# Softmax rows scaled on GpSimd: from a broadcast tensor operand to a per-partition scalar operand

## The reference

```
xn = layernorm(x)                                    # x: 4 x 512 x 256
s  = attention(xn)      # 16 heads of 128, 4 K/V heads, causal softmax, Wo, gelu, + xn, layer norm, gamma, beta
g  = silu(ffn(xn))      # gate and up 256 -> 1024, silu(gate) * up, down 1024 -> 256
out = x + s * g

scores = Q K^T / sqrt(128) + mask                    # mask: -1e9 above the diagonal
attn   = softmax(scores)                             # exp(scores - max) / sum
ctx    = attn V
```

## Time and profile before

| | |
|---|---|
| median of 3 runs | 715.47 us (715.37 to 715.48) |
| the profiled execution | 716.74 us |
| its span, first to last instruction | 714.9 us |
| PE busy | 671.6 us, 94% of the span |
| DVE / ACT / POOL busy | 480.0 / 433.2 / 279.7 us |
| granted TensorE clock, mean | 0.989 of full speed |

### The profile page before, as it was taken

One profiled execution on the slowest core, in us unless ns is written; L12 is line 12 of the kernel. 1 busy time (PEld: TensorE's weight loads), 2 busy tenths in 40 slices (PEclk: granted clock), 3 DMA queues, 4 the chain that ended last, 5 costly groups with the idle time before them and its releaser, 6 DMA issues.

```text
span 714.9 us, 11581 instructions
## 1 busy us (share of the span) xinstructions
PE 671.6 (94%) x3968; PEld 585.2 (82%) x3968; DVE 480.0 (67%) x1620; ACT 433.2 (61%) x1011; POOL 279.7 (39%) x328
## 2 busy tenths in 40 slices
PE   1889999999999999999999999999999999999982
PEld 1778888888888888897888888888888897888872
DVE  6764433334776777777868776786768677867777
ACT  3423232326767677668767675867767677767661
POOL 2599100000524324146815242484425146715234
PEclk9799999999999999999999999999999999999998
DMA  8334000002000000000110000002000000200000
GB/s 275 119 129 136 1 29 0 30 0 85 5 1 1 1 0 1 1 1 1 56 34 2 1 1 0 2 1 89 1 1 1 1 1 1 89 1 2 1 1 29
DMA packets 14503, 20.31 MB, mean 28 GB/s; under 512 B 752, under 2 KB 12144, under 8 KB 14192
## 3 DMA queue, kind: packets, MB, share of 16 engines
q1 hardware_dynamic: 13328, 14.37, 6.1%
q0 software_dynamic: 1120, 5.24, 2.2%
HBM read 15.41 MB, written 4.19 MB: 27 GB/s over the span
## 4 chain that ended last, share of the span: by engine, by line
PE 86%; DVE 7%; ACT 4%; issue 1%; DMA 1%; SPq 0%; DVEq 0%; ACTq 0%
PE bank L949 30%; PE down_ps L949 28%; PE down_ps L1048 8%; PE down_ps L987 6%; PE bank L974 6%; PE bank L976 6%; DVE cT_lo L822 2%; PE bank L1035 2%; ACT cT_hi L702 2%; DVE hidT_lo L766 1%; DMA raw<-in_wgu 1%; DVE pT_lo L804 1%; DVE xnT_lo L751 1%; ACT L655 1%; ACT res L655 0%
## 5 line engine op out<-in xcount | busy, mean ns | idle before, releaser
L561 POOL TENSOR_TENSOR probs<-probs,inv 128x512 f32<-128x512 f32 (+3 forms) x256 | 180.7, 720 | 385.0 <-DVE inv L907 384.9
L692 ACT ACTIVATE probs<-probs,least 128x512 f32<-128x512 f32 (+3 forms) x256 | 142.2, 558 | 40.5 <-DVE least L900 36.8
L900 DVE CUSTOM_DVE_ANT_0 probs<-bank,mask 128x512 f32<-128x512 f32 (+3 forms) x256 | 121.2, 486 | 12.1 <-issue 12.0
L804 DVE TENSOR_TENSOR pT_lo<-down_ps,pT_hi 128x512 fp32r<-128x512 f32 x156 | 107.1, 687 | 20.0 <-ACT pT_hi L698 15.4
L698 ACT ACTIVATE pT_hi<-down_ps 128x512 fp32r<-128x512 f32 x156 | 92.5, 593 | 33.1 <-PE down_ps L1048 31.1
L1048 PE MATMUL down_ps<-ident,probs 128*128 128x128 f32 x624 | 93.4, 272 | 0.0
L1048 PEld LDWEIGHTS down_ps<-ident,probs 128*128 128x128 f32 x624 | 75.5, 140 | 12.4
L949 PE MATMUL down_ps<-wo_lo,cT_hi 128*128 128x256 f32 x256 | 73.7, 288 | 6.0 <-DVE cT_lo L822 6.0
L816 DVE SCALAR_TENSOR_TENSOR qT_lo<-bank,bias,qT_hi 128x512 fp32r<-128x512 f32 x64 | 47.5, 750 | 43.5 <-ACT qT_hi L685 43.5
L949 PE MATMUL down_ps<-pT_lo,v_hi 128*128 128x512 f32 x156 | 67.8, 435 | 5.6 <-DVE cT_lo L822 4.2
L949 PE MATMUL down_ps<-wo_hi,cT_lo 128*128 128x256 f32 x256 | 72.0, 281 | 0.0
(11 more groups left out here) (139 smaller groups left out, 1547.6 us busy)
## 6 DMA issues: line engine op xcount, KB each, us to landing
x_row<-in_x SPq DMA_DIRECT2D x4, 512.0 KB, 6.8
raw<-in_wgu SPq DMA_DIRECT2D x4, 512.0 KB, 6.1
raw<-in_wq POOLq DMA_DIRECT2D x2, 1024.0 KB, 5.1
raw<-in_wo POOLq DMA_DIRECT2D x2, 1024.0 KB, 6.2
g_scratch<-g_out SPq DMA_DIRECT2D x4, 512.0 KB, 2.9
x_b<-in_x SPq DMA_DIRECT2D x4, 512.0 KB, 3.7
g_b<-g_scratch SPq DMA_DIRECT2D x4, 512.0 KB, 4.7
out<-res SPq DMA_DIRECT2D x3, 512.0 KB, 2.9
```

The costliest lines, as they stand in the source:

```text
L561: nc.gpsimd.tensor_tensor(p, p, inv[:, u % UNITS, g:g + 1].to_broadcast([P, (tile_of(u) + 1) * P]), ALU.mult).then_inc(probs_made, 1)
L692: nc.scalar.activation(p, p, ACT.Exp, bias=least[:, u % UNITS, g:g + 1], scale=-1.0, accum_out=total[:, u % UNITS, g:g + 1]).then_inc(exp_ ...
L804: nc.vector.tensor_tensor(lo[:], ps, f32(hi[:]), ALU.subtract).then_inc(probsT_split, 1)
L900: nc.vector.tensor_tensor_reduce(out=probs[t][:, g, :], in0=ps[:, 0:(t + 1) * P], in1=mask[:, (T - 1 - t) * P:], scale=-SCALE, scalar=BIG, ...
```

## The change

POOL's multiplication at L561 took `inv` as a second tensor of the same shape as the probabilities, a 128 x 1 column read again and again (`to_broadcast`). It becomes an instruction with one tensor input and `inv` as a scalar for each partition. Its place in POOL's list, its wait and its semaphore stay. Each of the 256 instructions changes in this way, and no other instruction of any engine.

```diff
                     p = probs[tile_of(u)][:, g, :]
-                    nc.gpsimd.tensor_tensor(p, p, inv[:, u % UNITS, g:g + 1].to_broadcast([P, (tile_of(u) + 1) * P]),
-                                            ALU.mult).then_inc(probs_made, 1)
+                    nc.gpsimd.tensor_scalar(p, p, inv[:, u % UNITS, g:g + 1], None, ALU.mult).then_inc(probs_made, 1)
```

## The result

The changed kernel takes 723.14 us in the median of 8 runs, the kernel before, timed beside it, 716.63 us (8 runs). The ratio is 1.0096 with a 95% interval of 1.0059 to 1.0132. The two sets of runs do not overlap: 722.1 to 728.7 us now, 715.4 to 721.1 before. The likeliest case of the prediction, no change at 715.5 us, was wrong; what happened is its rival 1, which had a chance of 0.38, and its range, 714.6 to 738, holds the time.

What follows compares the result with a forecast made beforehand. PE was taken to bound the kernel, POOL being in time by 0.18 us at twelve tile-3 transposes. All terms were 0: profiled 716.74 us + 0, which lies 1.27 over the median, so 715.5 us; range 714.6 to 738 us.

Steps and rivals of the forecast that it cites:

- likeliest case of the prediction: Whole kernel: POOL's multiplications get no dearer, nothing on the path changes, 715.5 us; chance 0.50.
- rival 1: Tile-3 transposes: PE waits for POOL if 512 columns cost over 1.29 us; 728.3 or 736.2 us; chance 0.38.
- the price of the new instruction: POOL's multiplication at L561, 512 columns: 0.62 us, or anything up to 1.04, taken from the CAST rows.
- The two bounds: POOL, 512 columns: 0.62 us from CAST rows; 1.90 from the two-tensor row, 1.29, plus 0.60 for the scalar's fetch.
- 12 places with 0.18 us of slack: First transposes of tile 3 (L1048): POOL ends 0.18 to 0.19 us ahead of the weight load in 12 of 16.
- POOL's work at a row end: Residual, root, eight output pieces at three earlier rows' ends: finish earlier, next first transpose has 0.18 us spare; term 0.
- A faster POOL gains nothing: POOL's multiplications: 68 us of busy time saved, none of it on the path; term 0.
- The threshold: Tile-3 places: 0.49 us of room for two heads' slip, so a 512-column instruction is free up to 1.29 us.
- Rival 2: POOL's multiplication: scalar adds 0.60 us fixed, columns 0.84 ns each, 512 columns 1.22 us; kernel 716.4 us; chance 0.08.
- Rival 3: Twelve tile-3 places: PE's records hide a wait, so sooner POOL gains at most 2.2 us, 713.3 us; chance 0.04.
- The signs named for rival 1: PE's 7.0 us wait for cT_lo shrinks, waits for POOL's probs appear at L1048, the chain gets a POOL share.
- The sign that engines touch each other: DVE's times would change beside a shorter POOL, a sign that the prediction's steps fail; no size given.

Runs made afterwards that it cites:

- ts_wide: Scalar operand for tile 3 only (64 of 256 instructions), the others keep the broadcast tensor; ratio to the kernel before 1.0085 (1.0062 to 1.0108).
- ts_narrow: Scalar operand for tiles 2, 1 and 0 only, tile 3 keeps the broadcast tensor; ratio to the kernel before 1.0027 (1.0003 to 1.0051).
- copy: Kernel before, with POOL copying the probabilities onto themselves instead of multiplying, normalisation left out; ratio to the kernel before 0.9987 (0.9955 to 1.0018).
- tt_three: Kernel before, with the 512-column broadcast multiplication cut into pieces of 256, 128 and 128 columns; ratio to the kernel before 1.0000 (0.9980 to 1.0021).

## Why the likeliest case of the prediction was wrong, and what was right

- **The step that failed is the price of the new instruction.** The text took "0.62 us, or anything up to 1.04" because "the row nearest to that is the CAST". It is 1.56 us. Reading one tensor fewer says little: POOL's copy costs 0.84 ns a column, its multiplication by the broadcast column 1.67, and its multiplication by a scalar 2.5 even with a constant. The two bounds, 0.62 and 1.90, did hold the price, and that is why the range held the time. The upper one did so partly by luck: it was built on 0.60 us for the fetch of the scalar, which takes 0.07 to 0.08, and on nothing for dearer columns, which are where the price went.
- **What bounds the kernel** was read rightly: PE, with POOL in no wait and no chain, but 12 places with 0.18 us of slack. All 12 late places are those, by ts_wide and ts_narrow. But the text says that behind POOL's work at a row end "the next row's first transpose there" has 0.18 us to spare. That first one has 3.00; the tight place is the one after it.
- **A faster POOL gains nothing:** shown by copy.
- **The threshold was right in kind and too low.** The text had a room of 0.49 us for two heads, so 1.29 us an instruction; the runs give 0.7, so about 1.04 + 0.35 = 1.39 us (tt_three, whose pair takes 2.62 us, so 1.31 a head, loses 0.3 us in the whole stretch). The semaphore took 0.053 us and not the 0.09 of DVE's row, and from load to load 0.55 us were recovered and not 0.40. The rows shown above give most of that difference. When PE is in time, the load of the transpose starts 0.10 us ahead of its matmul (278.48 and 278.58); when it is late, both start at 279.54. The text measured the room ahead up to the load and the room behind from the matmul, and so left these 0.10 out. From matmul to matmul 0.43 us are recovered (0.84 before, 0.41 now), near its 0.40.
- **Rival 1 with its own arithmetic.** With 1.56 us (0.52 more) and 0.61 at 128 columns (0.21 more), 9 x (1.06 - 0.49) + 3 x (0.21 + 2.09 - 0.41 - 0.49) = 5.1 + 4.2 = 9.3 us. The places cost 7.4. Twelve places with 0.2 us of room more would make it 6.9; the other 0.5 I can't divide among the terms. The recorded sum for rival 1 has two small slips: 5 x 0.60 - 0.41 is 2.59 and not 2.61, and 2 x 0.60 - 0.49 is 0.71 and not 0.72. It makes 728.2 instead of 728.3.
- **Rival 2** (dearer fixed part, cheaper columns) is wrong by the rows: the columns got dearer. **Rival 3** (a hidden wait) is wrong by copy: its stretch is 0.1 us shorter, where the rival had up to 2.2.
- **The signs named for rival 1** came: POOL in the chain, waits for probs at the transpose, and in the attention part PE's waits for cT_lo are 4.2 us in 4 places, where they were 7.0 us in 16. The sign that engines touch each other did not: DVE is busy for 480.9 us and was for 480.0.
```profile
PE down_ps L948 <- DVE cT_lo L821: 4.2, 4, 1.1
```

## What to carry to other kernels

An engine that is idle half the time and appears in no wait can still sit at 0.2 us from the bottleneck; measure, for each place where the busy engine takes its result, the time from the end of the one to the start of the other, and what idle time follows. Do not price an instruction by the number of tensors that it reads: on this engine take a row of the very operation, or test it alone. Moving work out of a full queue only helps if there is slack where it goes.

## What the hardware showed that I had not expected

GpSimd, 128 partitions, fp32, 512 columns: a copy 0.62 us, a multiplication by a broadcast column 1.04, by a whole tensor 1.29, by a constant as a scalar 1.50, by a scalar for each partition from memory 1.56. The two forms with only one tensor to read are the slowest of the four multiplications. The forms also start differently: where POOL waits for DVE's reciprocal, from its end to POOL's start it is 0.063 us with the copy, 0.080 with the broadcast column, 0.084 with the constant and 0.094 with the scalar from memory. And 69 to 80 ns for reading the scalar, on instructions that were beyond the room, cost 2.8 us of the stretch.
